# TensorE's order in an attention loop: the transposes of q and k directly behind the pre-score, and the second chunk of one step next to the first chunk of the following one

## The reference

```python
h = layernorm(x) + silu(cond) @ W_ada.T + b_ada
q, k, v = split(h @ Wqkv.T)                  # 16 heads of 64
q, k = layernorm(q), layernorm(k)            # over each head's 64
attn = softmax(q @ k.T / 8)
x = x + (attn @ v) @ Wout.T
gate = softmax(x @ Wgate.T)                  # 8 experts
# then, over all 4096 tokens: each expert takes its top 512 tokens by gate,
# LN -> fc1 (1024) -> gelu -> fc2 -> times the gate -> added to the token
```

## Time and profile before

| | us |
|---|---|
| three runs | 1189.59, 1192.31, 1192.90 |
| median | 1192.31 |
| profiled execution, own time | 1186.95 |
| its span | 1185.2 |
| TensorE busy | 1088.4 |
| VectorE busy | 793.0 |
| ScalarE busy | 774.3 |
| GpSimd busy | 556.1 |

### The profile page before, as it was taken

How to read it: one execution, slowest core, us unless ns; L and a number is a source line. 1 busy time by engine, 2 the same in 40 slices (tenths; PEclk the granted TensorE clock), 3 DMA queues, 4 the chain that set the end, 5 groups by cost and what they waited for, 6 DMA issues and landing times.

```text
span 1185.2 us, 24660 instructions
## 1 busy us (share of the span) xinstructions
PE 1088.4 (92%) x8355; PEld 841.6 (71%) x8355; DVE 793.0 (67%) x1616; ACT 774.3 (65%) x1458; POOL 556.1 (47%) x597
## 2 busy tenths in 40 slices
PE   6899999999999999999999999999994128999996
PEld 6667777777777777777777777777753026989995
DVE  5686767667675767676666757676655885777773
ACT  5787777868687878778687878787772004445541
POOL 2454545556464545455464645454561003454332
PEclk9999999999999999999999999999997567999998
DMA  5000000010100000000101000000004212554322
GB/s 177 19 10 19 19 19 19 18 35 0 35 18 18 18 18 18 18 18 18 35 0 35 18 18 18 18 9 19 11 19 161 49 57 71 150 153 126 107 26 28
DMA packets 31773, 48.60 MB, mean 41 GB/s; under 512 B 7920, under 2 KB 28528, under 8 KB 30448
## 3 DMA queue, kind: packets, MB, share of 16 engines
q1 hardware_dynamic: 25584, 39.49, 10.1%
q0 software_dynamic: 6144, 8.52, 3.9%
HBM read 35.29 MB, written 12.71 MB: 41 GB/s over the span
## 4 chain that ended last, share of the span: by engine, by line
PE 86%; DVE 7%; issue 2%; POOL 2%; ACT 2%; DMA 1%; SPq 0%; DVEq 0%; POOLq 0%; ACTq 0%
PE ch L487 14%; PE ch L489 12%; PE ch L488 12%; PE av L1392 10%; PE sc L1417 9%; PE sc L1408 6%; PE pq L1370 5%; PE av L1396 5%; PE mx L1430 2%; DVE hit L739 2%; PE sc L487 1%; PE sc L489 1%; PE sc L488 1%; PE ch L1444 1%; PE ch L1350 1%
## 5 line engine op out<-in xcount | busy, mean ns | idle before, releaser
L959 POOL TENSOR_TENSOR qk_lo<-qkT,qk_hi 128x512 fp32r<-128x512 f32 x128 | 169.5, 1324 | 259.4 <-ACT qk_hi L1038 236.6
L952 POOL TENSOR_TENSOR prob_sum<-prob 128x512 f32<-128x512 f32 x128 | 165.2, 1291 | 81.2 <-ACT prob L1065 81.0
L1222 DVE TENSOR_TENSOR av<-av,rec 128x256 f32<-128x256 f32 x128 | 55.1, 431 | 205.4 <-ACT rec L1061 200.5
L487 PE MATMUL ch<-w_hi,hT_lo 128*128 128x512 f32 x384 | 170.5, 444 | 1.1 <-DVE hT_lo L1215 1.1
L1241 DVE TENSOR_REDUCE m<-mx 128x4 bf16<-128x1024 f32 x128 | 155.4, 1214 | 0.0
L1065 ACT ACTIVATE prob<-sc 128x1024 f32<-128x1024 f32 x128 | 130.9, 1023 | 37.4 <-PE sc L1417 35.6
L489 PE MATMUL ch<-w_hi,hT_hi 128*128 128x512 f32 x384 | 151.7, 395 | 0.0
L488 PE MATMUL ch<-w_lo,hT_hi 128*128 128x512 f32 x384 | 151.5, 395 | 0.0
L1392 PE MATMUL av<-prob,V 128*64 128x256 f32 x1024 | 139.6, 394 | 6.3 <-DVE oT L1226 4.3
L866 DVE TENSOR_TENSOR qn<-raw,rstd 128x512 f32<-128x512 f32 x128 | 119.3, 990 | 32.7 <-POOL rstd L928 32.7
L964 POOL TENSOR_TENSOR o_lo<-oT,o_hi 128x256 fp32r<-128x256 f32 x128 | 101.1, 790 | 26.2 <-ACT o_hi L1070 26.2
(11 more groups left out here) (201 smaller groups left out, 2779.5 us busy)
## 6 DMA issues: line engine op xcount, KB each, us to landing
fcw<-experts SPq DMA_DIRECT2D x8, 2048.0 KB
x_sb<-x SPq DMA_DIRECT2D x16, 256.0 KB, 2.7
xr_sb<-x SPq DMA_DIRECT2D x16, 256.0 KB, 2.7
out<-tok SPq DMA_DIRECT2D x16, 256.0 KB, 2.2
rows_dram<-xh SPq DMA_DIRECT2D x16, 256.0 KB, 2.2
prob<-w_qk SPq DMA_DIRECT2D x2, 512.0 KB, 6.8
qn<-w_qk SPq DMA_DIRECT2D x2, 512.0 KB, 7.4
V<-w_vT SPq DMA_DIRECT2D x2, 512.0 KB, 7.3
```

What stands on the lines that cost most here:

```text
L487: nc.tensor.matmul(psum, l_lo, r_hi, start=first, stop=False)
L952: nc.gpsimd.tensor_tensor(prob_sum[(hp - 1) % 2][:, :, :], pr[:, :, 0, :], pr[:, :, 1, :], ALU.add).then_inc(prob_summed, 1)
L959: nc.gpsimd.tensor_tensor(qk_lo[par][:, :], qkT[par][:, :], qk_hi[par][:, :].bitcast(F32), ALU.subtract).then_inc(lo_ready, 1)
```

## The change

The block of four transposes leaves the head of a step and goes behind the pre-score of the step before, for the same pair (hp + 2, seen from there). Its two waits are counted accordingly. Second chunk (step hp) and first chunk (step hp + 1) are thereby next to each other where nothing else stands between.

```diff
                     live = (hp, 0) in CHUNKS and (cur if hp < 2 else nxt)
-                    if ahead:
-
-                        gpar, i = ((hp + 1) // GU) % 2, (hp + 1) % GU
-                        need(qn_ready, b * 2 + (hp + 1) // GU + 1)
-                        need(qk_evacuated, u + 1)
-                        for c, at in ((0, 0), (2, 1), (1, 2), (3, 3)):
-                            ins = nc.tensor.transpose(pq[:, at * P:(at + 1) * P], qn[gpar][:, c, i * P:(i + 1) * P], ident)
-                        ins.then_inc(qk_transposed, 1)
                     if live:
                         chunk(b, hp, 0)
...
                         ins.then_inc(pre_scored, 1)
+                    if (cur and nxt) or (cur and hp < UNITS - 2) or (nxt and hp >= UNITS - 2):
+
+                        gpar, i = ((hp + 2) // GU) % 2, (hp + 2) % GU
+                        need(qn_ready, b * 2 + (hp + 2) // GU + 1)
+                        need(qk_evacuated, u + 2)
+                        for c, at in ((0, 0), (2, 1), (1, 2), (3, 3)):
+                            ins = nc.tensor.transpose(pq[:, at * P:(at + 1) * P], qn[gpar][:, c, i * P:(i + 1) * P], ident)
+                        ins.then_inc(qk_transposed, 1)
                     if live:
                         chunk(b, hp, 1)
```

## The result

The changed kernel takes 1206.74 us (median of 4, 1204.0 to 1207.25), the kernel before 1190.95 us (median of 4): ratio 1.0128, 95% interval 1.0103 to 1.0153. Predicted was 1206.5 us, 14.2 us above the median shown then; measured are 15.8 us. Ratios, here and in the experiments, leave out executions in the chip's slow state, of which there was one: a run of the kernel before, of 1803 us, in the series of e1, e3, e4 and e6. The profiled execution took 1206.60 us with a span of 1204.8.

The account below looks back on a forecast made before the run. TensorE's own order was taken to set the pace, nothing waiting ahead of it. Twelve loop batches at +1.01 us (+12.1), with the other batches, gave +14.3 on the median of 1192.31: 1206.5 us, range 1195 to 1212.

Parts of the forecast that it names:

- Step A: TensorE's order at the junctions between steps becomes denser, as the drain behind the pre-score costs less: gain 0.045 us per junction.
- Steps B and C: Second chunk ends 0.39 us later, delaying qn; step 6's transposes wait 0.98 us at junction 6/7, cost 0.92 a batch.
- Step D: At step 2 the delayed high part comes too late for the pre-score: cost 0.27 us a batch, bounds 0 and 0.4.
- batch 0: No gate matmuls there; its attention waits hang on the same VectorE work and end 0.39 later: about +0.7 us.
- R1: Delay absorbed, as ScalarE catches up; qn and step 2 keep their times: +5 us in all, 1197.3; chance 0.14.
- R2: Faster: normalise ends before the transposes come at 6/7, so only the denser order's gain remains: 1188.0 us; chance 0.06.
- R3: New boundaries cost 0.09 us each, or marginal places open into stalls of 0.1 to 0.2 each: 1212 us; chance 0.07.

Follow-up runs that it names:

- e1: The changed kernel, but with the transposes of step 6 back behind the gate matmuls (junction 6/7 as before): 1194.21 us, ratio 1.0018 to the kernel before.
- e3: The changed kernel, same order, but the transposes of step 6 read a constant tile and need not wait for qn: 1191.11 us, ratio 1.0007 to the kernel before.
- e4: The kernel before with only junction 6/7 in the new order: 1197.45 us, ratio 1.0052.
- e6: The changed kernel, with GpSimd's qk_lo of step 6 made to wait until normalise is done: 1191.38 us, ratio 0.9997 to the kernel before.
- e5: The kernel before with only junction 4/5 in the new order, so only the second chunk of step 4 comes later: 1197.86 us, ratio 1.0073.
- e10: The kernel before, order unchanged, with only GpSimd's qk_lo of step 6 made to wait for normalise: 1190.17 us, ratio 0.9999.
- e8: The changed kernel with junction 1/2 back as before and GpSimd's qk_lo of step 6 behind normalise: 1188.56 us, ratio 0.9976 to the kernel before.
- e9: The changed kernel with GpSimd's qk_lo of step 6 behind normalise, and ScalarE evacuating step 2's pair ahead of chunk (1,1): 1186.71 us, ratio 0.9972 to the kernel before.
- e11: e9 with the junctions into step 0 and 0/1 of batch 0 left in the old order: 1186.87 us, ratio 0.9955 to the kernel before.
- e7: The kernel before with only junctions 0/1, 3/4, 5/6 and 7/0 in the new order, ScalarE and GpSimd untouched: 1189.16 us, ratio 0.9984.

## Why the prediction was right

**Place and sign.** The wait is where it was forecast: transposes of step 6 on L866, 16 times in all (one in the start-up, which was there before, and one in each of batches 0 to 14), with the gate matmuls behind them. e1 and e3 show that it is this wait and not the new order.

**Step A, the denser order.** Forecast 0.045 per junction, measured 0.05, and 0.08 at 0/1, where a chunk behind the output projection starts without the usual first bubble. The boundary that the trace of before did not show, chunk to chunk, costs the 0.24 of a normal pace, as the earlier trace rows suggested. The four junctions left gave 0.23, forecast 0.18. By the drain rule of the Trainium skill (TensorEngine Tiling, Key Properties) alone the gain would be 0, as the number of switches is the same; measured are 0.05 a place, so the visible price of a switch depends on what follows it.

**Steps B and C.** The late chunk delays its readers by 0.40 (forecast 0.39), the multiplies' end by 0.38. The wait is 0.92 (0.98), the cost over 4/5 to 6/7 is 0.99 - 0.05 - 0.05 = 0.89 (0.92). e4 gives the part of the bare move, 0.48. But the pass-through of exactly 0.39 was luck in part: e5 shows that the same delay, without chunk (5,1) late too, costs 0.91 at the end of the multiplies. I had taken L866 as a block of 4.12 us that moves as a whole. It is 2.48 us of work (its length in the start-up) and 1.64 of lost time beside GpSimd, 2.2 in e5. At least 1.1 of that is GpSimd's `qk_lo` alone, as e6 and e10 show (3.02), and the loss depends on who starts first.

**Step D.** Forecast 0.27, measured 0.29; e8 shows its cause by undoing 1/2. Its terms held too: 0.05 from the end of the high part to the pre-score, and 0.10 for its exposed first load.

**Sum.** A loop batch +0.95 (forecast 1.01), twelve of them 11.4 (12.1); batches 1 and 14 together 1.4 (1.6); batch 15 +0.1 (-0.1). The term that was mis-sized is batch 0: 3.21 us against 0.7. The forecast let its waits end 0.39 later. Measured were 0.21 and 0.43 in its first two steps, 1.21 in step 2/3 and 1.58 in 6/7. The last has the same root as e5: the fourth multiply now waits for qk_lo, L866 takes 3.92 instead of 2.84, the split of Wout and the division queue behind it, and TensorE waits 1.1 for qn and 1.4 for the division (1.00 before). e3 has 7.74 there without any wait for qn, as it waits 2.6 for the division instead; e6 6.24 without the GpSimd operation beside it. The 1.21 go with a longer stretch at the low clock (last section). That the total came within 0.3 us of 1206.5 is luck: batch 0 was taken 2.5 us too low, the loop and batches 1 and 14 together 0.9 too high, and the median from which the forecast started lies 1.4 above the one that four runs gave. The forecast's lower bound of 1201 for its own terms does not come out of its sum either: without step D, 14 times 0.27 us less, it is 1202.7.

**Rivals.** R1 (absorbed by ScalarE's earlier start) did not happen: ScalarE's idle time before L1032 is gone (54.3 us in the run before, 1.3 after), but it stands before the next chunk instead, and chunk (1,1) still comes late. R2 (no wait at 6/7) is what e6 brings about by a wait on GpSimd, by the road that R2 named: multiplies shorter by 1.1 us. R2's time of 1188.0 is not e6's 1191.38, because step D stays. R3's boundaries at 0.09 did not show. Of its small stalls one did, in one batch: in batch 1 step 3/4 takes 6.64 instead of 6.52, where the scores wait for VectorE's maximum.

**A sign that failed.** The prediction had the busy times of VectorE, ScalarE and GpSimd unchanged. ScalarE's moved by -3.0 and GpSimd's by +5.5 us, but VectorE's by +39.4. The forecast followed VectorE and GpSimd only where operations come later; it did not ask what the earlier `qk_lo` (step 0) would meet. That cost no time here, since nothing on TensorE's path waits there.

## What to carry to other kernels

When a saturated engine's order is changed, first list for each moved block the operand that arrives last and the spare time in its present place (here 0.46 us, filled by 0.91 us of gate matmuls), then what is delayed by being jumped over, and follow that delay to the next tight margin; gains of 0.05 a place don't pay for one lost margin. A chain that crosses VectorE and GpSimd doesn't shift as a block: ask which of their operations will now start first, and keep long GpSimd work out of a critical run of two-input VectorE operations. Moved in the four harmless places alone the same change gains 0.16%, and with one wait on GpSimd and an earlier evacuation on ScalarE it gains 0.3 to 0.45% (e9 and e11, whose intervals overlap).

## What the runs showed of the hardware

**The granted clock behind an idle stretch.** In batch 0 TensorE waits 3.3 to 3.4 us for the division, and the clock falls to its lower level (0.50, 1.2 of 2.4 GHz). How long it stays there differs. Stretches (length, busy PE, PEld, DVE, ACT, POOL, clock) of before, after and e11, each from the wait on:

```profile
44.00:48.30 4.30, 1.04 (x9) 0.82 (x8) 4.15 (x9) 0.12 (x2) 1.66 (x1) 0.94 0.00 0
48.30:51.20 2.90, 2.90 (x13) 1.49 (x14) 2.73 (x5) 2.81 (x7) 0.00 (x0) 0.51 0.00 0
51.20:53.00 1.80, 1.80 (x22) 1.43 (x21) 0.61 (x2) 1.47 (x4) 1.28 (x2) 1.00 0.00 0
```

```profile
48.80:51.60 2.80, 2.76 (x12) 1.39 (x13) 2.65 (x5) 2.71 (x7) 0.00 (x0) 0.50 0.02 6
51.60:54.10 2.50, 2.50 (x20) 1.97 (x20) 1.20 (x4) 1.26 (x3) 1.85 (x2) 0.50 0.00 0
```

```profile
48.50:51.00 2.50, 0.53 (x4) 0.41 (x6) 2.35 (x6) 0.64 (x2) 0.00 (x0) 0.73 0.00 0
51.00:56.00 5.00, 5.00 (x32) 3.21 (x28) 3.21 (x7) 3.51 (x9) 1.95 (x2) 0.50 0.02 3
```

Before, the clock was back at 51.2, 2.9 us after work resumed; in the changed kernel it was still at 0.50 at 54.1, and in e11 until 56. Step 2/3 of batch 0 took 5.15, 6.36 and 6.53 us accordingly. The twelve traces fall into two groups by their record of the granted clock:

| low stretch in batch 0 | traces | step 2/3 of batch 0 |
|---|---|---|
| 3.4 us | before, e3, e4, e5, e7, e9, e10 | 5.15 to 5.74 |
| 6.8 us | after, e1, e6, e8, e11 | 6.30 to 6.53 |

The length of the wait doesn't order them: e8 and e9 both waited 3.4 us and are in different groups. Whether a kernel always falls into the same group isn't shown, as each has one trace. About 1 us of a single profiled execution hangs on it.

**GpSimd against VectorE.** A 128x512 multiply of VectorE with two SBUF inputs takes 0.68 us alone and 1.77 to 1.78 when it starts just behind a GpSimd operation of 1.3 us. GpSimd's are stretched too (o_lo 1.17 to 1.18 beside the multiplies, 0.74 elsewhere). Near a tie a few hundredths decide, as far as GpSimd's rough record times can tell: in batch 0 of the kernel before, qk_lo's record starts 0.03 ahead of the fourth multiply, and there the multiply takes 0.68 and qk_lo 1.84; in batch 1 it starts 0.04 ahead, and the multiply takes 1.79 and qk_lo 1.28.
